# A pipelined cross-attention and FFN kernel: the first chunk's steps fourteen beats ahead, two of its products in halves

## What is computed

```python
x = x + tanh(g_xattn) * cross_attention(layernorm(x), ctx)     # 16 heads of 32, softmax over 154 keys
h  = float_quantize(relu(layernorm(x) @ w1.T + b1), 4, 3)      # 2048 hidden units
y  = float_quantize(h @ quantize(w2).T + quantize(b2), 5, 10)
x = x + tanh(g_ffn) * y
```

## Time and profile before

| | us |
|---|---|
| median of three runs | 1588.99 |
| lowest, highest | 1588.32, 1590.34 |
| profiled execution, its own time | 1590.96 |
| its span, first to last instruction | 1589.2 |
| PE busy, share of the span | 1532.4, 96% |
| DVE busy | 948.6, 60% |
| POOL busy | 878.5, 55% |
| ACT busy | 813.0, 51% |

### The profile page before, as it was taken

How to read it: one execution, slowest core, us unless ns; L and a number is a source line. 1 busy time by engine, 2 the same in 40 slices (tenths; PEclk the granted TensorE clock), 3 DMA queues, 4 the chain that set the end, 5 groups by cost and what they waited for, 6 DMA issues and landing times.

```text
span 1589.2 us, 23580 instructions
## 1 busy us (share of the span) xinstructions
PE 1532.4 (96%) x8576; PEld 692.9 (44%) x8576; DVE 948.6 (60%) x1297; ACT 813.0 (51%) x1196; POOL 878.5 (55%) x919
## 2 busy tenths in 40 slices
PE   7875999999999999999999999999999999999998
PEld 4422444444444444444444444444444444444443
DVE  7778465674756566574656657574665757445231
ACT  3665564545545564555546455554645455455421
POOL 3688365564736556474655547464654746445310
PEclk9997999999999999999999999999999999999999
DMA  8356363453544454344445444344543534333120
GB/s 335 97 158 149 116 160 110 134 119 112 111 132 104 117 135 109 105 107 149 101 116 137 116 99 115 124 103 130 134 115 103 120 113 104 102 98 86 44 54 27
DMA packets 252855, 186.70 MB, mean 117 GB/s; under 512 B 160012, under 2 KB 209476, under 8 KB 251076
## 3 DMA queue, kind: packets, MB, share of 16 engines
q1 hardware_dynamic: 252740, 185.19, 43.7%
HBM read 99.95 MB, written 51.59 MB: 95 GB/s over the span
## 4 chain that ended last, share of the span: by engine, by line
PE 75%; DVE 11%; POOL 6%; issue 5%; ACT 2%; DMA 1%; SPq 0%; DVEq 0%; ACTq 0%
PE ring L514 53%; PE ring L708 8%; PE m_ps L616 4%; DVE y L1014 4%; PE s_ps L646 2%; PE y_ps L674 2%; DVE bns L1039 2%; DVE resid L1056 2%; DVE xn L1065 1%; PE d_ps L663 1%; POOL x L1149 1%; POOL rs L1161 1%; POOL pmain L1123 1%; DMA resid<-in_w_t 1%; PE s_ps L639 1%
## 5 line engine op out<-in xcount | busy, mean ns | idle before, releaser
L514 PE MATMUL ring<-late_a,w 128*128 128x512 f16 x3072 | 703.1, 380 | 7.2 <-issue 7.2
L514 PEld LDWEIGHTS ring<-late_a,w 128*128 128x128 f16 x3072 | 299.0, 98 | 347.3 <-issue 17.4
L815 ACT ACTIVATE late_b<-ring,b_sb,wsc 128x512 fp8e4<-128x512 f32 x256 | 199.4, 779 | 396.7 <-PE ring L514 396.7
L1123 POOL TENSOR_TENSOR pmain<-p,pmain 128x512 f16<-128x512 f32 x256 | 302.0, 1182 | 176.3 <-ACT p L793 173.2
L992 DVE TENSOR_REDUCE smax<-m_ps 128x4 f32<-128x616 f32 x256 | 203.4, 794 | 226.7 <-PE m_ps L616 226.5
L1014 DVE RECIPROCAL y<-d_ps 128x256 f32<-128x256 f32 x128 | 223.4, 1745 | 64.2 <-PE d_ps L666 61.9
L793 ACT ACTIVATE p<-s_ps,prob_log,sc 128x512 f32<-128x512 f32 x320 | 247.9, 775 | 1.0 <-POOL pleft L1123 1.0
L708 PE MATMUL ring<-w,late_b 128*128 128x512 fp8e4 x1024 | 228.5, 379 | 5.6 <-DVE ffn L1023 3.8
L790 ACT ACTIVATE pmain<-s_ps,prob_log,sc 128x512 f16<-128x512 f32 x256 | 198.1, 774 | 5.9 <-PE s_ps L646 5.8
L1123 POOL TENSOR_TENSOR pleft<-p,pleft 128x512 f16<-128x512 f32 x64 | 76.5, 1195 | 182.0 <-ACT p L793 182.0
L514 PE MATMUL ring<-wo,yT 128*128 128x512 f16 x768 | 175.0, 381 | 0.0
(11 more groups left out here) (149 smaller groups left out, 1424.0 us busy)
## 6 DMA issues: line engine op xcount, KB each, us to landing
qstack<-q_rows SPq DMA_DIRECT2D x192, 128.0 KB, 3.0
pstack<-left_rows SPq DMA_DIRECT2D x192, 128.0 KB, 2.6
xin<-in_x SPq DMA_DIRECT2D x64, 256.0 KB, 3.4
q_rows<-qparts SPq DMA_DIRECT2D x32, 512.0 KB, 2.8
left_rows<-pleft SPq DMA_DIRECT2D x64, 256.0 KB, 2.5
resid<-in_x SPq DMA_DIRECT2D x64, 256.0 KB, 3.2
out_x<-resid SPq DMA_DIRECT2D x64, 256.0 KB, 2.7
resid<-in_w_t SPq DMA_DIRECT2D x5, 1024.0 KB, 6.2
```

Source lines behind the costliest of these rows:

```text
L514: last = pe.matmul(dst, lhs(a, k), rhs(b, k), start=(k == 0 and p == 0), stop=(k == n_k - 1 and p == 2))
L815: nc.scalar.activation(hT[:, j, :], ring_bank("h", c, j)[:], ACT.Relu, bias=b1_sb[:, j:j + 1], scale=wsc[:, j // 4, 1:2], saturate=False). ...
L1123: nc.gpsimd.tensor_tensor(part[:, 1, :], p32[:, n % 2, :], part[:, 0, :], ALU.subtract).then_inc(prob_lo, 1)
```

## The change

All chunk 0 steps get their own tables, about fourteen beats earlier than before, on every engine; the loop starts at beat -26 instead of -12. The tables of chunk 1 for ranking and shift go (it takes the steady beats 18 to 33), its other tables are moved. The steps of the start (keys, values, conversions of weights) are moved earlier with chunk 0. Chunk 0's attention is then in beats -14 to 14, its projection in 19 to 23, its hidden products from 24 on, spread up to beat 58, and its products with w2 in 62 to 68. Chunk 1's attention stays in beats 28 to 56, and all later chunks stay where they were. Hidden products 0 and 1 of chunk 0 are made in two halves of 256 rows (`hidden_half`): the first halves of both wait only for tiles 0 and 1, the second halves for tiles 2 and 3.

```diff
-FIRST, LAST = -12, 70
+FIRST, LAST = -26, 70
+HIDDEN_HALVES = {0: 24, 1: 25, 2: 26, 3: 28}
-MAX_OWN = {0: [-12, -11, -10, -9, -8, -7, -6, -5, -4, -3, -2, -1, 0, 1, 2, 3], 1: [18, 19, 20, 21, 22, 23, 24, 25, 27, 29, 30, 30, 33, 34, 38, 39]}
-SHIFT_OWN = {0: [-4, 4], 1: [26, 42]}
-LN1_STAT_OWN = {1: [-1, 1, 3, 5]}
-LN1_APPLY_OWN = {1: [1, 4, 6, 7]}
-XSPLIT_OWN = {1: [3, 7, 11, 11]}
-Q_OWN = {1: [16, 17, 21, 27]}
-SPLIT_Y_OWN = {0: [12, 16, 25, 30]}
-O_OWN = {0: [33, 35, 36, 37]}
-LN2_OWN = {0: [35, 36, 37, 38]}
-X2TURN_OWN = {0: [36, 39, 39, 39]}
+MAX_OWN = {0: [-26, -25, -24, -23, -23, -21, -20, -20, -20, -15, -14, -13, -13, -12, -11, -11]}
+SHIFT_OWN = {0: [-18, -8]}
+LN1_STAT_OWN = {1: [-11, -11, -10, -8]}
+LN1_APPLY_OWN = {1: [-6, 0, 0, 3]}
+XSPLIT_OWN = {1: [-5, 3, 4, 6]}
+Q_OWN = {1: [13, 16, 18, 20]}
+LEFT_OWN = {0: [-14, -7, 0, 7]}
+MAIN_OWN = {0: [-13, -12, -11, -10, -6, -5, -4, -3, 1, 2, 3, 4, 8, 9, 10, 11]}
+LEFT_AWAY_OWN = {0: [-15, -7, 3, 13]}
+LEFT_BACK_OWN = {0: [-14, -6, 4, 16]}
+VALUE_OWN = {0: [-7, 0, 7, 14]}
+NORMAL_OWN = {0: [-7, -5, 1, 3, 9, 9, 13, 14]}
+SPLIT_Y_OWN = {0: [-2, 3, 10, 15]}
+O_OWN = {0: [19, 21, 22, 23]}
+LN2_OWN = {0: [21, 22, 23, 24]}
+HIDDEN_OWN = {0: [27, 29, 31, 34, 34, 36, 37, 38, 39, 44, 49, 51, 52, 55, 57, 58]}
+FFN_OWN = {0: [62, 65, 67, 68]}
+X2TURN_OWN = {0: [22, 22, 23, 24]}
...
-KV_STEPS = {4: [-4, -4, -3, -2], 5: [-1, 1, 1, 2], 6: [3, 5, 5, 6], 7: [5, 5, 6, 7], 8: [8, 8, 9, 9], 9: [9, 10, 10, 11], 10: [11, 12, 12, 12], 11: [14, 15, 15, 16], 12: [18, 19, 19, 19]}
+KV_STEPS = {4: [-19, -18, -18, -17], 5: [-14, -14, -12, -10], 6: [-11, -9, -9, -8], 7: [-9, -9, -8, -7], 8: [-6, -6, -6, -6], 9: [-5, -5, -4, -4], 10: [-3, -3, -3, -2], 11: [0, 3, 3, 4], 12: [1, 3, 3, 4]}
-GATE_AT = {0: -4}
-W_FOLD = {0: 1}
-WO_HI = {0: 15}
-WO_LO = {0: 18}
-W1_HI = {0: 11, 1: 20, 2: 24, 3: 30}
-W1_LO = {0: 13, 1: 26, 2: 26, 3: 38}
-W2_LOAD = {0: 27, 1: 47, 2: 49, 3: 53}
-W2_PART = {0: 43, 1: 49, 2: 52, 3: 56}
+GATE_AT = {0: -26}
+W_FOLD = {0: -10}
+WO_HI = {0: -9}
+WO_LO = {0: -5}
+W1_HI = {0: -1, 1: 5, 2: 10, 3: 11}
+W1_LO = {0: 0, 1: 12, 2: 12, 3: 25}
+W2_LOAD = {0: 19, 1: 40, 2: 41, 3: 51}
+W2_PART = {0: 33, 1: 41, 2: 45, 3: 55}
...
+            def hidden_half(n):
+                half, j = divmod(n, 2)
+                if j == 0:
+                    for landed in x2t_in:
+                        pe.wait_ge(landed, (half + 1) * 2 * DMA)
+                if n == 0:
+                    pe.wait_ge(w1_ready, W1_ORDER.index(0) + 1)
+                if half == 0:
+                    ring_free("h", 0, j)
+                cols = slice(half * HALF_COLS, (half + 1) * HALF_COLS)
+                last = product(ring_bank("h", 0, j)[:, cols], lambda a, k: w1[:, 0, a, k, j * P:j * P + P],
+                               lambda b, k: x2T[:, b, k, cols], KT)
+                if half:
+                    last.then_inc(hid_done, 1)
...
-                run(hidden, HIDDEN_AT, beat)
-                run(ffn_out, FFN_AT, beat)
+                once(hidden_half, HIDDEN_HALVES, beat)
+                run(lambda c, j: hidden(c, j) if c or j > 1 else None, HIDDEN_AT, beat, HIDDEN_OWN)
+                run(ffn_out, FFN_AT, beat, FFN_OWN)
```

More of the change, by code:

```diff
@@ L303, in build @@
             steps_of(KV_STEPS, lambda n, k: ring_jobs.append(("kv", 0, n)) if k == 0 else None, beat)
-            for kind, at, own in (("q", Q_AT, Q_OWN), ("o", O_AT, O_OWN), ("h", HIDDEN_AT, {}),
-                                  ("f", FFN_AT, {})):
+            for kind, at, own in (("q", Q_AT, Q_OWN), ("o", O_AT, O_OWN), ("h", HIDDEN_AT, HIDDEN_OWN),
+                                  ("f", FFN_AT, FFN_OWN)):
                 run(lambda c, k: ring_jobs.append((kind, c, k)) if (kind, c) != ("q", 0) else None, at, beat, own)
@@ L502, in _ @@
                 run_batch(keys_stacked, KST_AT, beat)
[L503 removed]
+                run(store, STORE_AT, beat, STORE_OWN)
                 once(w2_load, W2_LOAD, beat)
@@ L868, in _ @@
                 run(lambda c, m: query_hi(c, m) if c else None, Q_AT, beat, Q_OWN)
-                run(relu, HIDDEN_AT, beat)
+                run(relu, HIDDEN_AT, beat, HIDDEN_OWN)
                 run(lambda c, t: x_hi(c, t) if c else None, XSPLIT_AT, beat, XSPLIT_OWN)
```

48 lines of the change are left out of this document (24 added, 24 removed).

## The result

The changed kernel took 1605.07 us (median of four runs, 1603.89 to 1607.34) against 1589.66 for the kernel before beside it. The ratio is 1.0099, 95% interval 1.0087 to 1.0111: one per cent slower, where 12 us faster was forecast. The profiled execution's span is 1602.1 us, 12.9 more than the 1589.2 before.

What follows compares the result with a forecast made beforehand. PE bounds nearly all but the start, where idle and slow time cap the gain at 41 us. Terms 31.6 + 37.8 + 42 + 31 + 64 = 206.4 us against 218.8: gain 12.4, 1577 us, range 1560 to 1590.

Steps and rivals of the forecast that it cites:

- stage D: Second halves to beat 56, chunk 1's fourth value product: PE-bound, 59.7 us of work plus 4 of waits, 64 (60 to 87).
- beats 56 to 70: After chunk 1's fourth value product: all as before but for hidden products, so no change in time.
- Stage A: From 31.6 us, beat loop just begun, to chunk 0's first value product: nearly the old order, 37.8 us (36 to 40).
- Stage B: Chunk 0's first to fourth value product: POOL tightest, 39.2 us busy plus 3 of waits, 42 us (39 to 50).
- a fourth value after 119: Sign that the prediction is wrong: chunk 0's fourth value product, expected near 111 us, comes after 119.
- Stage C: Chunk 0's fourth value product to the second halves: latency of its normalisation, projections and layer norm 2, 31 us (26 to 38).
- old stage D: Kernel before, 161.6 us (chunk 0's first hidden product) to 211.0 (chunk 1's fourth value): PE busy 49.4 us, no idle time.
- credit of 7.8 us: At beat 56, 14 of chunk 0's hidden products done instead of 11; three at 2.60 us, so old 211.0 counts as 218.8.
- 5.1 us of slow products: Start of the kernel before: three products at low clock, 1.9 + 1.8 + 1.4 us, counted in the 41 us ceiling.
- rival (3): Slower: ACT and POOL, not PE, set chunk 1's attention in stage D; 11 us slower, 1600; chance 0.13.
- Rival (2): Idle time only moves, DVE and POOL queues setting the pace: sum 215.4, gain 3 us, 1586; chance 0.17.
- the 76 us: Sign that the prediction is wrong: stage D, forecast at 64 us, takes over 76.

Runs made afterwards that it cites:

- e2_start: Changed kernel with its first beats ordered as in the kernel before, 14 beats earlier: 1600.53 us, ratio 1.0059 to the kernel before.
- e3_filler: Changed kernel with chunk 0's hidden products 1 to 15 at other beats, one between each two ranks of chunk 1: 1603.17 us, ratio 1.0081.
- e14_after_short: Changed kernel with the maximum of chunks 0 to 2 over 16 of 154 keys per head, part of the work left out: 1595.20 us, ratio 1.0036.
- e4_pure: Kernel before with all steps of chunk 0 and of the weights 14 beats earlier, chunk 1 as before, products whole: 1633.95 us, ratio 1.0273.
- e8_pure_spread: e4_pure with chunk 0's hidden products, products with w2 and stores at the changed kernel's beats: 1623.46 us, ratio 1.0206.
- e11_w1late: e7_halves with the low part of w1's last block on DVE at beat 42 instead of 38: 1585.28 us, ratio 0.9960.
- e6_lead7: Kernel before with chunk 0 and the weights 7 beats earlier, chunk 1 as before, whole products: 1627.65 us, ratio 1.0234.
- e7_halves: Kernel before with only chunk 0's hidden products 0 and 1 in halves, at beats 39 to 42: 1587.30 us, ratio 0.9978.
- e1_whole: Changed kernel with hidden products 0 and 1 of chunk 0 whole again, at beats 27 and 29: 1603.93 us, ratio 1.0085.
- e5_pairs: Kernel before with the 16 ranks of each of chunks 2 to 15 in 8 pairs, two in one beat: 1716.43 us against 1591.36, one run.

## Why the prediction was wrong

The place was right: nothing changed before 31.6 us or after beat 70, and all of the difference is in the stages named. The sum failed, and the step that failed most is the term of stage D: "I add 4 us of waits: 64" measured 72.8 us. The sum had 206.4 us for beat 56, against an old 218.8; the profile has 227.5. The 25.3 us between the forecast gain of 12.4 and the measured loss of 12.9 divide so:

| step | forecast, us | measured | off by |
|---|---|---|---|
| A, "nearly the old order" | 37.8 | 43.0 (38.6 to 41.8 in three other profiles of this order) | 5.2 |
| B, POOL-bound | 42 | 44.9 | 2.9 |
| C, to the second halves | 31 | 35.0 | 4.0 |
| D, "4 us of waits" | 64 | 72.8 | 8.8 |
| beats 56 to 70, "all is as before" | 0 | 4.4 | 4.4 |

Stage A: the step "in nearly the old order" failed. I read the tables for what they contain and not for what follows what. Three ranks in one beat were visible in the diff, and the round trip of a rank was in the old trace. e2_start restores the order of the start and brings 3 to 6 us back: that the order costs is shown. Of the profile's 5.2 us, though, over 3 are a granted clock of 0.76 from 41 to 55 us, which two of four profiles have; the stage in the other two is 0.8 and 1.3 us over the forecast.

Stage B: the mechanism held. POOL was busy 41.7 of 44.9 us, against 39.2 of 42 forecast, and PE idled 14.0 us where I had 16. I counted no more stretched instructions than before; the groups show more of them among the probabilities and the splits of y, and fewer among those of x. PE's work was 30.9 us against some 26, one query product at a low clock in it. That this stage had lost its products (chunk 1's queries) I saw and priced as idle time inside a stage that ends earlier. It ended at the same time as before, 119.46 against 119.89, with A 5.2 and B 2.9 us over. That was one of the signs of being wrong that the prediction names: a fourth value after 119.

Stage C: the chain was as described, with the first projection after 9.7 us instead of 7.4, the first halves 26 us after the value and not 23, and the second halves 9.1 us behind those and not 7.6.

Stage D was the term that was mis-sized most. PE's work was 63.1 us against 59.7, and the waits 9.7 instead of 4. Of the work, 2.3 us are a low clock (2.10 us for a half product instead of 1.47, 4.44 for a whole one instead of 2.75). Of the waits, 7.9 us are for the maximum. I had compared with the old stage D, in which PE never waited, but there 11 hidden products stood beside some 10 ranks, and here 14 beside 17. It is tempting to blame the round trip of the ranks, and the runs speak against it as the whole cause. With a product between each two of chunk 1's ranks (e3_filler) the waits moved and the time stayed; with the short maximum (e14_after_short) D was only 1.1 us shorter. What they show in its place is 9.7 us of idle time that moves from wait to wait when the ranks or the maximum change, and little of which goes. What sets the length of D, in DVE, ACT, POOL or their order, stays open.

The credit of 7.8 us for three products done early was not all a gain either: beats 56 to 70 then had 3.6 us idle, and two products there ran at a low clock (6.67 us for the pair at 241.25 instead of 5.34). e4_pure and e8_pure_spread show the same at full size: the hidden products can fill one stretch or the other.

The clock: the forecast let 5.1 us of slow products vanish with the idle time. Low clock moved with the idle time instead, to the query products, the hidden product at 222.94 and the f32 products of the start; the mean granted clock was 0.988 against 0.987, and busy time rose by 4.3 us.

The rivals: rival (3) had the sign and the place, stage D, at 1600, but not the cause. ACT was busy 48.3 of D's 72.8 us and POOL 39.2, PE's waits for them there were 1.8 us, and D took less than the 76 us that I gave as a sign of it. Rival (2), idle time only moves, was nearer in mechanism: the table of idle times is its picture, with 8.6 us more at the end of the move than at its start. I gave the two together 0.30.

The Trainium skill (GPSIMD Engine Reference, 1. Specifications) says that GpSimd shares its SBUF interfaces with VectorE and contends with DVE instructions of two SBUF inputs. The trace agrees again in e11_w1late: with the long two-input DVE instruction gone from beside it, the subtraction took 1.15 us instead of 2.54. I had put no gain on moving one such instruction; it was worth 1.3 us of wait there, since that tile ended PE's gap.

What stays open: why the clock falls early in stage A in some executions; what sets the length of stage D; which of the collisions of chunk 0 with chunk 1 make up e6_lead7's 37 us; and whether some placing of ranks and products makes a lead pay. Of the nine kernels with a lead that do the whole work, e2_start was the best, and it was still 0.6% behind.

## What to carry to other kernels

A lead given to the first item of a pipeline doesn't add work for the bound engine; it only moves it, and every product that fills an early wait is missing from a later one. So count idle time over all stages up to the steady state before crediting a gap that closes. Read a new order for neighbours: an instruction that waits for a round trip through another engine needs work of at least that length ahead of it, in each place where it stands. Cut a stage finer before you blame an order for its length: a mean clock over 40 us hid a dip of 14 us that was most of the difference. And of a change with two parts, try each alone: here the small one, two products in halves, was worth 0.2% and the large one cost 0.85% (e7_halves and e1_whole).

## What the runs showed of the hardware

A pair of 128x308 matmuls, a maximum over 128x616 on DVE out of the same PSUM banks and the next pair repeat every 1.41 us; PE idles 0.98 us of that, and 112 such pairs cost 125 us (e5_pairs). With a maximum over 128x64 they repeat every 0.84 us, with 0.41 us idle (e14_after_short). Twelve matmuls of 256 columns take 1.47 us against 2.75 for 512 columns, so two halves are 2.94 us; no run's time shows the 0.19.

The granted clock falls without a long gap. In the changed kernel one 97x512 matmul at 108.10 us took 0.61 us instead of 0.39, and the clock was 0.50 from 108 to 112 us; PE's idle times just before were 1.15, 1.75 and 0.95 us, and it had been busy 1.40 us of the last four. And one list of instructions can meet two clocks: 0.76 or 1.00 from 41 to 55 us, in two profiles each, which was worth 3.3 us.
